# Routing rows to expert regions chunk by chunk, instead of one sort after all logits, in both mixture-of-experts feed-forward stages

## The reference

```python
logits = jnp.einsum('btd,ed->bte', x, router_w)
top_vals, top_idx = jax.lax.top_k(logits, K)
top_w = jax.nn.softmax(top_vals, axis=-1)
...
h = jnp.einsum('nd,edh->enh', xf, w1)
h = jnp.square(jax.nn.relu(h))
y = jnp.einsum('enh,ehd->end', h, w2)
...
out = jnp.einsum('nk,nkd->nd', w_f, y_sel)
```

## Time and profile before

| | us |
|---|---|
| median of 3 runs | 1259.72 (1250.94 to 1259.96) |
| the profiled execution | 1259.48 |
| its span, first to last instruction | 1257.8 |

### The profile page before, as it was taken

The page is one execution under the profiler, slowest core; times in us unless marked ns, Lnnn a source line. Parts: engine busy times, 40 slices in busy tenths (PEclk is TensorE's granted clock), DMA queues, the critical chain, the costliest instruction groups (busy, mean ns, idle before and its releaser), DMA issues. The chain is left out here.

```text
span 1257.8 us, 21544 instructions
## 1 busy us (share of the span) xinstructions
PE 1032.9 (82%) x6452; PEld 856.7 (68%) x6484; DVE 745.7 (59%) x1608; ACT 602.3 (48%) x1552; POOL 606.7 (48%) x608
## 2 busy tenths in 40 slices
PE   3746999999956688888898888989836999999960
PEld 3735999999944466666676666666525999999950
DVE  6974444444437868687878786865355444444437
ACT  1323555555523464656465656465314555555530
POOL 6923555555431345464545454648502555555520
PEclk9998999999986799999999989999858999999985
DMA  7872222322223111111111110000061223233339
GB/s 227 277 298 74 76 77 76 99 77 77 72 56 93 38 30 42 43 43 42 43 43 51 34 43 13 26 9 26 26 268 51 86 95 97 97 96 96 97 115 321
DMA packets 73066, 111.68 MB, mean 89 GB/s; under 512 B 10616, under 2 KB 60288, under 8 KB 71680
## 3 DMA queue, kind: packets, MB, share of 16 engines
q1 hardware_dynamic: 48704, 60.48, 14.4%
q0 software_dynamic: 13632, 37.24, 9.3%
q10 hardware_dynamic: 10624, 12.58, 3.0%
HBM read 66.50 MB, written 43.78 MB: 88 GB/s over the span
## 5 line engine op out<-in xcount | busy, mean ns | idle before, releaser
L427 POOL DMA_INDIRECT ys_d<-xs,row_of x142 | 140.8, 992 | 192.0 <-DVE xs L811 186.3
L491 ACT ACTIVATE hs<-pH 128x512 f32<-128x512 f32 x142 | 85.0, 599 | 226.3 <-PE pH L613 226.3
L422 POOL DMA_INDIRECT xs<-xn_d,token_of x142 | 138.2, 974 | 113.1 <-DVE token_of L785 70.4
L800 DVE TENSOR_TENSOR xl<-pT,xh 128x256 fp32r<-128x256 f32 x142 | 60.3, 425 | 217.6 <-ACT xh L504 217.3
L805 DVE TENSOR_TENSOR h2l<-hs,h2h 128x512 fp32r<-128x512 f32 x142 | 98.4, 693 | 76.8 <-ACT h2h L499 76.7
L1604 DVE SCALAR_TENSOR_TENSOR acc<-bank,cwh,acc 128x511 f32<-128x511 f32 (+2 forms) x120 | 89.7, 747 | 43.5 <-ACT acc L1218 40.6
L633 PE MATMUL pY<-w2h,h2h 128*128 x568 | 102.0, 302 | 0.6 <-DVE h2l L805 0.4
L1122 POOL TENSOR_TENSOR yv<-yv,sz 128x512 f32<-128x512 f32 x32 | 40.7, 1273 | 118.7 <-DVE yv L1643 115.5
L613 PE MATMUL pH<-w1h,xh 128*128 x284 | 91.5, 404 | 1.8 <-DVE xl L800 1.1
L613 PE MATMUL pH<-w1l,xh 128*128 x284 | 91.0, 402 | 0.0
L633 PE MATMUL pY<-w2h,h2l 128*128 x568 | 89.8, 280 | 0.0
(11 more groups left out here) (250 smaller groups left out, 2554.9 us busy)
## 6 DMA issues: line engine op xcount, KB each, us to landing
m_yg<-ys_d SPq DMA_DIRECT2D x64, 128.0 KB, 2.1
xs<-ys_d SPq DMA_DIRECT2D x12, 512.0 KB, 6.5
wst<-in_L_ffn_w_dram ACTq DMA_DIRECT2D x8, 512.0 KB, 4.8
xs<-in_L_attn_x_dram SPq DMA_DIRECT2D x8, 512.0 KB, 6.1
hs<-in_L_ffn_w_dram ACTq DMA_DIRECT2D x8, 512.0 KB, 4.8
xn_d<-xs SPq DMA_DIRECT2D x8, 512.0 KB, 3.4
lo_d<-w1l SPq DMA_DIRECT2D x1, 4096.0 KB, 11.8
lo_d<-w2l SPq DMA_DIRECT2D x1, 4096.0 KB, 21.4
```

Of the source, the lines that this page charges most:

```text
L422: pool.indirect_dma_start(out=xg[:, t % NX, :], out_offset=None, in_=xn_d, in_offset=bass.IndirectOffsetOnAxis(ap=token_of[:, t:t + 1], ax ...
L427: pool.indirect_dma_start(out=ys_d, out_offset=bass.IndirectOffsetOnAxis(ap=row_of[:, t:t + 1], axis=0), in_=y[:, t % NX, :], in_offset=No ...
L491: act.activation(r[:, u, :], pH[u][:, :], ACT.Relu).then_inc(relu_done.sem, 1)
```

## The change

Each expert gets a region of 8192 rows in a DRAM tensor `xs_d`. As soon as the logits of a group of four chunks are known, DVE picks the two experts of each token (`pick_two`), numbers the rows within their experts (`number_group`), PE adds counts over partitions (`count`), DVE computes the slots (`place_group`), and POOL scatters the normalised rows to their regions, two indirect transfers per chunk; `xn_d` is gone. Rows are 272 floats: 256 values, then the result row number and the first expert. A table per group (`table`) lists the tiles of 128 rows that have become full; after the last group it lists the partly filled ones, whose gaps are filled by `fill_hole`. The tile loop is still 71 tiles, but loads them with a plain transfer on SP's queue at a row number read from the table; only the results are scattered by POOL.

Synchronisation and queues of the FFN, SP first. `load_lo` moves to ACT's queue and the spill of the low weights moves into the first tile loop. The last stage's loads take both results of a token in one run.

```diff
+        def group_for(t):
+
+            return min((t + AG * TOP - 1) // (AG * TOP), G)
+
+        def window(g):
+
+            if g == G:
+                return FULL, NL
+            return max(0, (g - 1) * AG * TOP + 1), g * AG * TOP + 1
...
+            def fetch(t):
+
+                if t >= NX:
+                    sp.wait_ge(g_split.sem, g_split.done(t - NX))
+                row = sp.value_load(row_at[0:1, t:t + 1], min_val=0, max_val=E * REG - P)
+                sp.dma_start(xg[:, t % NX, :], xs_d[bass.ds(row, P), 0:XW]).then_inc(gathered[t % NX].sem, 16)
...
-            def load_lo(m):
-
-                n = E * WCOLS // NA
-                for i, w in enumerate((w1l, w2l)):
-                    sp.dma_start(w[:, m * n:(m + 1) * n].bitcast(F32), lo_d[i, :, m * n:(m + 1) * n]).then_inc(w_loaded[i], 16)
...
-                sp.dma_start(lo_d[0], w1l[:, :].bitcast(F32)).then_inc(w_spilt, 16)
-                sp.dma_start(lo_d[1], w2l[:, :].bitcast(F32)).then_inc(w_spilt, 16)
...
+                    sp.wait_ge(tabled, g + 1)
+                    if first and g < G:
+                        sp.wait_ge(landed[g], 16 * TOP * AG)
+                    if g == G:
+                        sp.wait_ge(holes_filled, 16 * E * (1 if first else 2))
+                        if first:
+                            sp.wait_ge(hollow_stored, 16 * (NL - FULL))
...
-                    for k in range(TOP):
-                        sp.dma_start(er[n % NE][:, k, :, :], tiles(ys_d, n * EG * P + (1 + k * T) * P)).then_inc(e_loaded[n % NE].sem, 16)
+                    for m in range(EG):
+                        i = n * EG + m
+                        sp.dma_start(er[n % NE][:, m, :, :], by_token(ys_d, i * P, P)).then_inc(e_loaded[n % NE].sem, 16)
```

```diff
-            def lo_weights(n):
-                pool.wait_ge(w_hi.sem, w_hi.done(n))
-                pool.tensor_tensor(wlo(n), wraw(n), whi(n).bitcast(F32), ALU.subtract).then_inc(w_lo.sem, 1)
...
+            def scatter_x(g):
+                pool.wait_ge(placed.sem, placed.done(g))
+                for m in range(AG):
+                    for k in range(TOP):
+                        pool.indirect_dma_start(out=xs_d, out_offset=bass.IndirectOffsetOnAxis(ap=r["slots"][:, g % 4, k, m:m + 1], axis=0),
+                                                in_=xa[:, (g * AG + m) % NXA, :], in_offset=None).then_inc(landed[g], 16)
...
+            if first:
+                pows(0)
+                pows(1)
+                pows(2)
+                for g in range(G):
+                    scatter_x(g)
+                    if g + 3 < G:
+                        pows(g + 3)
...
+                if t in HOLE_AT:
+                    if t == HOLE_AT[0]:
+                        pool.wait_ge(holes_known, 1)
+                    fill_hole(HOLE_AT.index(t))
```

```diff
-            for piece in range(C // PC):
-                u = piece % 2
-                act.wait_ge(oh_hi.sem, oh_hi.done(piece))
...
+                    for half in range(2):
+                        n = 2 * g + half
+                        hi_weights(n)
+                        if n + NRAW - 1 < NW:
+                            load_weights(n + NRAW - 1)
+                        copy_xT(g * AG + 2 * half)
+                        copy_xT(g * AG + 2 * half + 1)
+                        if g + 1 < G:
+                            norm((g + 1) * AG + 2 * half)
+                            norm((g + 1) * AG + 2 * half + 1)
+            else:
+                n = E * WCOLS // NA
+                for i, w in enumerate((w1l, w2l)):
+                    for m in range(NA):
+                        act.dma_start(w[:, m * n:(m + 1) * n].bitcast(F32), lo_d[i, :, m * n:(m + 1) * n]).then_inc(w_loaded[i], 16)
...
+            def spill(n):
+                i, m = n % 2, n // 2
+                act.dma_start(lo_d[i, :, m * WCOLS:(m + 1) * WCOLS], wlo(n).bitcast(F32)).then_inc(w_spilt, 16)
```

PE of the FFN:

```diff
+            def count(g):
+                pe.wait_ge(numbered.sem, numbered.done(g))
+                pe.wait_ge(placed.sem, placed.done(g - 2))
...
+                pe.wait_ge(placed.sem, placed.done(G - 1))
+            else:
+                pe.wait_ge(w_loaded[0], 16 * NA)
...
+                if t == 0 and not first:
+                    pe.wait_ge(w_loaded[1], 16 * NA)
```

DVE of the FFN takes over the low weights:

```diff
+            def lo_weights(n):
+                dve.wait_ge(w_hi.sem, w_hi.done(n))
+                dve.tensor_tensor(wlo(n), wraw(n), whi(n).bitcast(F32), ALU.subtract).then_inc(w_lo.sem, 1)
...
+            def table(g):
+
+                t0, t1 = window(g)
+                n, s0, own = t1 - t0, g * E, (g + 1) * E
...
+                    link(dve.tensor_scalar(pages[:, g + 1, :], keep["tots"][:, g, :], PAGE_BITS, None, ALU.bitwise_and))
+                link(dve.tensor_tensor(fresh[:, :], pages[:, g + 1, :], pages[:, g, :], ALU.subtract))
+                link(dve.tensor_tensor_scan(ends[:, own + 1:own + E + 1], ones8[:, :], fresh[:, :], ends[:, own:own + 1], ALU.mult, ALU.add))
+                dve.tensor_tensor(less[:, own:own + E], ends[:, own:own + E], pages[:, g, :], ALU.subtract)
...
+                link(dve.tensor_scalar(expert_i[:, t0:t1], row_at[:, t0:t1], REG.bit_length() - 1, WCOLS.bit_length() - 1, ALU.logical_shift_right, ALU.logical_shift_left))
+                dve.tensor_copy(expert_f[:, t0:t1], expert_i[:, t0:t1]).then_inc(tabled, 1)
...
+                shift(0)
+                for g in range(G):
+                    if g + 1 < G:
+                        moments(g + 1)
+                    lo_weights(2 * g)
+                    if g + 1 < G:
+                        shift(g + 1)
+                    for m in range(AG):
+                        pick(g * AG + m)
+                    number(g)
+                    lo_weights(2 * g + 1)
+                    place(g)
+                    if g >= 2 and g - 2 < 3:
+                        table(g - 2)
+            else:
+                for g in range(3):
+                    table(g)
...
+                if t in (0, *(window(g)[0] for g in range(G + 1))):
+                    dve.wait_ge(tabled, group_for(t) + 1)
+                dve.wait_ge(gathered[t % NX].sem, gathered[t % NX].done(t // NX))
+                dve.scalar_tensor_tensor(row_of[:, t:t + 1], xg[:, t % NX, D + 1:D + 2], expert_f[:, t:t + 1], xg[:, t % NX, D:D + 1], ALU.not_equal, ALU.add)
...
+                if t in TABLE_AT:
+                    table(3 + TABLE_AT.index(t))
```

The helpers that both blocks call, and the constants:

```diff
+def pick_two(dve, link, keep, r, i, scores):
+
+    best = keep["best"][:, i, :]
+    link(dve.max(best, scores))
+    return dve.max_index(r["idx"][:, i % AG, :], best, scores)
+
+
+def number_group(dve, link, keep, r, g, rows):
+
+    oh, buf = r["oh"], r["buf"]
+    link(dve.tensor_copy(r["idf"][:, :, :], r["idx"][:, :, 0:TOP].rearrange("p c k -> p k c")))
+    dve.tensor_copy(rows[:, :, D:D + 1].rearrange("p c a -> p (c a)"), keep["token2"][:, g * AG:(g + 1) * AG])
+    dve.tensor_scalar(rows[:, :, D + 1:D + 2].rearrange("p c a -> p (c a)"), r["idf"][:, 0, :], float(WCOLS), None, ALU.mult)
+    link(dve.tensor_tensor(oh[:, :, :, :].rearrange("p k c e -> p (k c) e"),
+                           keep["iota_e"][:, :].rearrange("p (a e) -> p a e", a=1).to_broadcast([P, TOP * AG, E]),
+                           r["idf"][:, :, :].rearrange("p k (c a) -> p (k c) a", a=1).to_broadcast([P, TOP * AG, E]), ALU.is_equal))
+    link(dve.tensor_tensor(buf[:, :, 1:AG + 1].rearrange("p e c -> p c e"), oh[:, 0, :, :], oh[:, 1, :, :], ALU.add))
+    return dve.tensor_tensor_scan(r["pre"][:, :, :].rearrange("p e c -> p (e c)"), keep["first_col"][:, :, :].rearrange("p e c -> p (e c)"),
+                                  buf[:, :, :].rearrange("p e c -> p (e c)"), 0.0, ALU.mult, ALU.add)
+
...
+def place_group(dve, link, keep, r, g, counts):
+
+    oh, prod = r["oh"], r["prod"]
+    for k in range(TOP):
+        last = dve.tensor_tensor(prod[:, k * AG:(k + 1) * AG, :], oh[:, k, :, :], counts[:, :, 0:AG].rearrange("p e c -> p c e"), ALU.mult)
+    link(last)
+    link(dve.tensor_reduce(r["red"][:, :, :].rearrange("p k c -> p (k c)"), prod[:, :, :], AX.X, ALU.add))
+    dve.tensor_copy(r["buf"][:, :, 0:1], r["pre"][:, :, AG:AG + 1])
+    dve.tensor_tensor(keep["tots"][:, g, :], counts[:, :, AG:AG + 1].rearrange("p e a -> p (e a)"), keep["base"][:, :], ALU.add)
+    return dve.scalar_tensor_tensor(r["slots"][:, g % 4, :, :].rearrange("p k c -> p (k c)"), r["idf"][:, :, :].rearrange("p k c -> p (k c)"), float(REG),
+                                    r["red"][:, :, :].rearrange("p k c -> p (k c)"), ALU.mult, ALU.add)
...
+EARLY_AT, EARLY_HI, EARLY_LO, EARLY_OUT = (21, 44), (24, 48), (28, 52), (56, 58, 60, 62)
+TABLE_AT, HOLE_AT, GATES_AT = (2, 10, 18, 26, 34, 42), tuple(range(45, 53)), 60
```

(39 more changed lines are left out.)

622 lines of the change are left out of this document (281 added, 341 removed).

## The result

The changed kernel takes 1293.76 us (median of 4 runs, 1288.38 to 1296.94) against 1259.84 for the kernel before: 1.0275 times, interval 1.0222 to 1.0327. It is slower, by 34 us where 16 were forecast. The profiled execution has a span of 1291.1 us, 33.3 more than before.

A forecast was written before the change was run, and what follows sets the result against it. It took both exposed sorts ahead of the tile loops as the object, with routing moved into busy phases. 0.5 + 25.4 + 18.8 − 26.6 + 3 − 5 = +16.1 on 1259.48 gave 1275.6 us; 80% range 1243 to 1305.

The forecast's parts named there:

- loops: Both FFNs' tile loops: tables and `row_of` cost nothing under DVE's idle time; uncovered, 18 + 14 us per FFN.
- the first block's end and Mamba's start: From the first FFN's last `down` to Mamba's first `mask`: forecast unchanged, 0 us.
- Mamba's end: Behind POOL's last root in Mamba: sixteen exposed scatters, 20.0 us, plus 3 of landing; +18.8 us (14 to 22).
- the last stage: After the second FFN's tile loop: loads of both results in 2 KB runs go faster; −5 us (−10 to 0).
- Mamba's body: Mamba's slots: exposed `number`, pick and `count`, 2.8 us a group, plus 5.8 for tail scatters; +25.4 us (+8 to +47).
- First phase: First FFN's logits phase: sort goes, DVE groups take 12.0 us with a wait through ACT; +0.5 us (−21 to +22).
- The rival (9.3, DVE without waiting): First FFN's logits phase: DVE needs 9.3 us a group without waiting, −21 us, total 1254; chance 0.18.
- Second FFN's start: Ahead of the second FFN's first `down`: no sort, low weights decide, 24.8 us instead of 51.4; −26.6 us (−29.6 to −21).
- Contention: Rival in Mamba: copies and two-input operations of `number` and `place` meet POOL operations; body +63 us, total 1313; chance 0.12.
- Holes: Tile loops: loads from tile 57 on wait for the last hole, 1.5 us in each FFN; +3 us (0 to 8).

## Why the prediction was wrong, point by point

The direction was right, and so were the two largest exchanges. The size was off by 17.2 us: loops +11.0 more than forecast, the first block's end and Mamba's start +6.2, Mamba's end +4.6, the last stage +4.5, Mamba's body −8.3, the rest −0.8. That Mamba's body came out cheaper is luck for the sum: without it the miss would have been 25.5.

- **First phase: right to 0.7 us, and for the reason given.** A group of 12.0 was forecast, 11.96 is there, with the turn through ACT ahead of the third pick. The rival (9.3, DVE without waiting) fell. The scatters on POOL were hidden, but not all at the speed foreseen: "no more than 0.2 an issue" came from a trace in which no indirect issue begins within a DVE tensor operation of over 1 us. Seven of the eight that begin within `lo_weights` took 1.33 to 1.62, against 0.960 in the median. The Trainium skill's rule (SBUF — State Buffer, "DVE blocks DMA") speaks of DVE copies. Beside the short copies here (up to 0.33) an issue took 0.96 unless it also met `lo_weights`, so what the trace shows is a wait for two-input operations.
- **The tile loops: the step that failed.** "The tables and `row_of` in the tile loop ... I cost at nothing: DVE is idle over 1 us in each tile". The idle time is there, 1.33 us ahead of `split_x`, but a table is one piece of 2.64, and within one tile only what fits ahead of the next split is free. The excess makes the tile 0.84 longer, at the last table 1.7: (5 × 0.84 + 1.7) × 2 = 11.8 of the 14.0 by which both loops grew. PE's waits for the split are 8.7 of it. In parts 9.6 of the 14.0 went. The right comparison was a piece's length with the slack of one turn, not the work's sum with the loop's idle time.
- **POOL's drain: a term that was missing.** The trace of before has it, as a drain of 3.65 and 6.10 us of idle POOL at the block's end, and I took the block's end as fixed. It grew by 5.47 after the first FFN and adds 5.27 after Mamba. Two earlier drains took 8.2 off the way from the first loop to Mamba at no cost; Mamba's own drain stayed, 4.0 to 4.5 after 48 transfers in the runs that move the last scatters.
- **Mamba's end: the mechanism right, one part short.** 20.0 us for the sixteen scatters were forecast and measured, 3 of landing against 1.7; the drain made the rest.
- **Second FFN's start: right to 0.1.** The low weights decide, 24.6 from their first request to the first `down`. The figure is closer than its working: 21.4 and 2.5 make 23.9, and the other 0.9 of the 24.8 has no row.
- **Mamba's body: right in place, too high in size.** `number` does cost its own time ahead of the mask with s mod 4 = 3 (1.2 to 1.5 us in six of eight groups, 3.3 in the last, whose slot also has the tail's scatters, 10.9 in all), but slots with s mod 4 = 0 got 9.2 shorter, which I hadn't counted, while those with 3, where `place` and a scatter pair stand, got 13.3 longer. In sum 17.1 against 25.4, inside the range given; the profile with the earlier drains, at the same clock of 0.95, gives 16.2. The 10.9 is 10.9 to 11.6 in all seven profiles that have this order of the lists, whatever the clock. The −9.2 is not such a price: it runs from −1.6 (clock 0.93) to −13.8 (0.97), and is −7.2 in the second profile of the kernel before itself. "The other slots have the room ... and take pick and scatters for nothing" was too simple for POOL. In a slot with s mod 4 = 3 of after it has no gap ahead of `decay_state`:

```profile
756.99 0.20 POOL L1167 TENSOR_TENSOR hc<-hc,m_ht 128x5 f32<-128x5 f32 x1
757.36 1.08 POOL L1153 DMA_INDIRECT xs_d<-m_xn,m_slots  x1 [0.17 <-issue]
758.74 0.96 POOL L1153 DMA_INDIRECT xs_d<-m_xn,m_slots  x1 [0.30 <-issue]
759.72 1.05 POOL L1126 TENSOR_TENSOR S<-S,dts 64x512 f32<-64x512 f32 x1
760.72 1.27 POOL L1131 TENSOR_TENSOR yv<-yv,xD 128x512 f32<-128x512 f32 x1
764.50 1.26 POOL L1136 TENSOR_TENSOR yv<-yv,sz 128x512 f32<-128x512 f32 x1 [2.51 <-DVE yv L1691]
```

  Its idle 2.51 us stands only behind `add_skip` (L1131). Whether that placing costs anything is what stayed open above; DVE's waits for `add_skip`, 4.6 us at two places here and 2.3 at one in the second profile of the changed kernel, are gone with the scatters behind it, so by that wait it costs a few us at most.
- **Contention: out.** The copies in Mamba's `number` take 0.17 to 0.18 in the median:

```profile
L856 DVE CAST m_idf<-m_idx x8: 171/172/619, 561.9 to 952.2; 128x8 f32<-128x8 uint32 x8
L857 DVE COPY m_xn<-token x8: 171/182/966, 562.1 to 952.4; 128x4 f32<-128x4 f32 x8
```

  Three of these sixteen were longer, 0.54, 0.62 and 0.97. Each ended with the POOL operation on whole rows beside it (L1145, L1146). The Trainium skill's rule (SBUF — State Buffer, "Who interferes with whom") agrees with these three. Most of the others ran at 0.17 to 0.19 beside POOL's `powers` (L1120), which the rival had counted like any tensor operation. Its price was also summed wrongly: 9 was taken off as counted already, but 7 × (2.05 − 1.4) = 4.6 was.
- **Holes: 0 instead of +3.** No tile from 57 on is longer than 3.48; the last holes land in time.
- **Last stage: −0.5 instead of −5.** I divided all bytes by the best rate. DVE's 64 operations come in eight groups of 3.25, 26 in all, behind 5.7 us until the first load is there and ahead of 3.7 for the last store: 35.4 is the floor, and the 39.3 measured leave 4 us of waits between groups. The stage still waits for its loads, between the groups 3.9 us after and 4.7 before, so the longer runs changed little.

## What to carry to other kernels

Work that is put into a pipelined loop is free only as far as one piece of it fits into the slack of one turn; compare these two, and cut the piece where it doesn't fit. When a stage is spread over the stages ahead of it, look at what stands behind the last of them on each queue (here 20 us of scatters, and POOL's drain): here that part could go into the next block, but there only at a point where no large load is under way. Before a few us between two versions are put down to an edit, compare executions at the same granted clock. With these repairs, and `number` in a slot with room, the same idea takes 0.9884 (0.9805 to 0.9964) of the old time instead of 1.0275, a difference of under 2%.

## What the runs showed of the hardware

A drain on POOL took about 0.1 us for each indirect transfer issued since the drain before: 0.86 after 10, 1.02 after 12, 5.17 after 48, 5.37 after 50, 7.81 after 80, 8.20 after 85 in the first FFN; 4.0 to 4.5 after 48 and 5.27 after 64 at Mamba's end; 6.51 after 79 and 7.8 after 95 at the end of the second FFN. A block's end counts as one, and all engines wait there. With more transfers since the last drain this doesn't hold: 142 left 3.65 (the kernel before), 143 left 9.12 (the changed one), and 120 left 2.66 in Mamba's block with the scatters doubled; what holds there wasn't tried.

An indirect issue on POOL that begins while DVE is within `mask` or `lo_weights`, tensor operations of 1.2 us with both inputs in SBUF, waits for its end: 25 of 25 end 0.83 to 0.93 us behind it, and the longest took 2.10 instead of 0.96.

And the granted clock over the masks of Mamba, where PE is busy for 86 to 88% of the time, varied between 0.93 and 0.97 from run to run in seven profiles of the same loop, and their span between 486.2 and 470.8 us.
